# A macaron block in float32 on one core: the attention pass in another order, with other PSUM banks and other places for its transfers

## The reference

```
x = x + 0.5 * ffn(layernorm(x))
x = x + attention(layernorm(x))
x = x + 0.5 * ffn(layernorm(x))

attention, 16 heads of 32:
  q, k = l2_normalize(x Wq), l2_normalize(x Wk);  v = x Wv
  alpha = sigmoid(x Wa + ba);  beta = sigmoid(x Wb + bb)
  for each token:  pred  = state^T k
                   state = alpha * state + k (beta * (v - pred))^T
                   out   = state^T q
  y = rmsnorm(out) * g_norm * silu(x Wg);  return y Wo

ffn, 64 slots:
  h = gelu([x, mean of slots] w1 + b1);  logits = (h w2 + b2) / (|tau| + 0.1)
  weights = softmax over the 8 largest logits, 0 elsewhere
  slots' = GRU(slots, weighted means of x);  out = weights (slots' wv + bv) wo + bo
```

## Time and profile before

| | |
|---|---|
| time, median of 3 runs | 3005.53 us (2997.7 to 3006.02) |
| the profiled execution itself | 2985.76 us |
| its span in the trace | 2983.5 us |
| PE / PEld / DVE / ACT / POOL busy | 91% / 65% / 63% / 35% / 44% |
| mean granted TensorE clock, 1 being 2.4 GHz | 0.961 |
| DMA traffic | 224.78 MB, 75 GB/s on average; 277585 of 365966 packets under 512 bytes |
| largest lines of the chain that ended last | L849 22%, L1052 8%, L906 7%, L1011 5%, L1033 5% |

### The profile page before, as it was taken

How to read it: one execution, slowest core, us unless ns; L and a number is a source line. 1 busy time by engine, 2 the same in 40 slices (tenths; PEclk the granted TensorE clock), 3 DMA queues, 4 the chain that set the end, 5 groups by cost and what they waited for, 6 DMA issues and landing times.

```text
span 2983.5 us, 117215 instructions
## 1 busy us (share of the span) xinstructions
PE 2726.1 (91%) x51052; PEld 1952.7 (65%) x51052; DVE 1869.4 (63%) x5306; ACT 1041.1 (35%) x1962; POOL 1326.6 (44%) x1767
## 2 busy tenths in 40 slices
PE   7999789999999999999999999999999999999877
PEld 6887466666666666666666666666666666666653
DVE  7777456665666666666656666656666666665536
ACT  5776223333333333333233333333333333333320
POOL 2221344554444545444454555544544444455410
PEclk9999899999999999999999999999999999999978
DMA  7342122222112222221222222221212222122168
GB/s 232 94 160 64 37 53 60 61 61 61 40 55 56 61 61 61 61 61 50 52 61 57 57 61 61 61 61 43 55 52 61 61 61 57 52 54 61 49 240 310
DMA packets 365966, 224.78 MB, mean 75 GB/s; under 512 B 277585, under 2 KB 294033, under 8 KB 365457
## 3 DMA queue, kind: packets, MB, share of 16 engines
q1 hardware_dynamic: 356240, 200.51, 23.9%
q10 hardware_dynamic: 9216, 16.78, 1.5%
HBM read 125.49 MB, written 74.97 MB: 67 GB/s over the span
## 4 chain that ended last, share of the span: by engine, by line
PE 81%; DVE 10%; issue 5%; ACT 2%; DMA 1%; SPq 1%; POOL 1%; DVEq 0%; ACTq 0%; POOLq 0%
PE psum L849 22%; PE psum L1052 8%; PE psum L906 7%; PE psum L1011 5%; PE psum L1033 5%; PE psum L970 4%; PE psum L946 4%; PE psum L1020 4%; PE psum L1073 4%; PE psum L690 3%; DVE blk L2627 2%; PE psum L989 2%; PE psum L753 2%; DVE blk L2629 2%; PE psum L927 2%
## 5 line engine op out<-in xcount | busy, mean ns | idle before, releaser
L849 PE MATMUL psum<-w_all,xnT 128*128 128x512 f32 (+2 forms) x2048 | 774.8, 509 | 3.0 <-ACT xnT L1715 2.4
L2064 POOL TENSOR_TENSOR sm<-sm,half 128x1 f32<-128x1 f32 (+1 forms) x384 | 535.4, 1394 | 72.9 <-ACT sm L1759 56.9
L849 PEld LDWEIGHTS psum<-w_all,xnT 128*128 128x128 f32 x2048 | 364.8, 195 | 147.2 <-issue 97.4
L2627 DVE TENSOR_TENSOR blk<-blk 128x30 f32<-128x30 f32 (+14 forms) x960 | 375.4, 391 | 49.5 <-issue 23.9
L2629 DVE TENSOR_TENSOR blk<-blk 128x30 f32<-128x30 f32 (+14 forms) x960 | 351.6, 366 | 33.0
L906 PEld LDWEIGHTS psum<-xnT,w_all 128*128 128x128 f32 x2048 | 262.4, 206 | 49.2 <-issue 47.5
L906 PE MATMUL psum<-xnT,w_all 128*128 128x128 f32 x2048 | 280.2, 294 | 3.2 <-issue 3.2
L1033 PE MATMUL psum<-qg,st 32*32 32x64 f32 x8192 | 186.8, 232 | 98.6 <-DVE st L2646 95.2
L1020 PE MATMUL psum<-pk,uw 32*32 32x64 f32 x8192 | 226.0, 217 | 34.2 <-issue 33.1
L1052 PE MATMUL psum<-w_out,gate 128*128 128x512 f32 x512 | 250.7, 612 | 0.4 <-DVE gate L2651 0.4
L2163 POOL TENSOR_TENSOR sq<-sq 128x256 f32<-128x256 f32 x64 | 47.4, 741 | 453.8 <-ACT sq L1795 453.8
(11 more groups left out here) (278 smaller groups left out, 4738.1 us busy)
## 6 DMA issues: line engine op xcount, KB each, us to landing
blk<-n_scratch SPq DMA_DIRECT2D x64, 512.0 KB, 4.7
xin<-in_L_attn_x_dram SPq DMA_DIRECT2D x96, 256.0 KB, 3.1
n_scratch<-nn SPq DMA_DIRECT2D x64, 256.0 KB, 3.8
xh<-xc SPq DMA_DIRECT2D x64, 256.0 KB, 2.7
e_scratch<-blk SPq DMA_DIRECT2D x32, 512.0 KB, 2.7
E<-e_scratch SPq DMA_DIRECT2D x64, 256.0 KB, 3.9
x_scratch<-xh SPq DMA_DIRECT2D x62, 256.0 KB, 2.1
rxn<-in_L_attn_x_dram SPq DMA_DIRECT2D x32, 256.0 KB, 3.0
```

Source lines behind the costliest of these rows:

```text
L849: last = mm(dst, xnT[b][:, k * P:(k + 1) * P], w_all[:, k * WK + at:k * WK + at + n], start=(k == 0), stop=(k == KC - 1))
L2064: return g.tensor_tensor(dst, a, half[:, 0:n], ALU.pow)
L2627: own(tt(o, Y[:, 0:rows, s_:s_ + 1].to_broadcast([P, rows, cols]), N[:, s_:s_ + 1, s_ + 1:CH].to_broadcast([P, rows, cols]), ALU.mult))
```

## The change

The functions compute the same as before, with the same instructions. Three things are replaced.

- **The table of PSUM banks**, and with it the condition in every `free(...)` of TensorE's functions.
- **The order of the calls** in `step_pe`, `step_act`, `step_dve`, `step_pool` and in the `first_...` and `last_...` lists. The small products of a tile are spread differently among the large ones, and `apply_uw` of the second batch begins in the step before, beside that of the first.
- **The order of the transfers** in `step_sp`.

```diff
-        ffn_at = [banks(0, 1), banks(7, 1)]
-        xT_at = [banks(6, 1), banks(3, 1)]
-        k_at = [banks(4, 1), banks(2, 1)]
...
+        ffn_at = [banks(1, 1), banks(0, 1)]
+        xT_at = [banks(7, 1), banks(7, 1)]
+        k_at = [banks(4, 1), banks(0, 1)]
...
             def out_proj(n, b, part):
                 if part == 0:
                     pe.wait_ge(S["y3"], both(n, b))
                     if b == 0:
-                        free((n + 1, (S["e4"], n + 1)), (n - 1, (S["top"], both(n - 1 + NT, 0))), (n, (S["gate"], both(n, 1))))
+                        free((n + 1, (S["draw"], both(n + 1, 0))), (n, (T["qg"][0], nth(n, 1))))
...
             def logits(n, b):
                 pe.wait_ge(S["hT"], both(n + NT, b))
...
-                    free((n + 2, (S["xnT"], both(n + 2, 0))), (n + 1, (S["vb"], both(n + 1, 1))), (n, (T["qg"][1], nth(n, 1))))
+                    free((n + 2, (S["qn"], both(n + 2, 1))), (n, (S["ysq"], both(n, 1))))
...
             def step_sp(o, p, q, r, s):
-                load_first(p, 0)
-                inverse_in(r, 0)
-                inverse_in(r, 1)
-                coupling_out(q, 0)
+                store_second(r, 0)
+                hold(q, 0)
+                store_alpha(s)
                 load_first(p, 1)
-                coupling_out(q, 1)
-                store_second(r, 0)
-                coupling_in(q)
-                hold(q, 0)
                 store_second(r, 1)
+                load_alpha(o)
                 hold(q, 1)
                 inverse_out(q)
-                store_alpha(s)
-                load_alpha(o)
+                inverse_in(q, 0)
+                inverse_in(q, 1)
+                coupling_out(p, 0)
+                coupling_out(p, 1)
+                load_first(o, 0)
+                coupling_in(p)
```

More of the change, by code:

```diff
@@ L1133, in last_pe @@
                 apply_uw(NT - 2, 1, 3)
+                out_proj(NT - 2, 0, 3)
+                slots(NT - 3)
                 apply_gy(NT - 2, 1, 3)
-                slots(NT - 3)
-                qe_T(NT - 2, 1, 1)
                 apply_gy(NT - 2, 1, 4)
@@ L1235, in last_pe @@
                 apply_uw(NT - 1, 1, 3)
+                out_proj(NT - 1, 0, 3)
+                slots(NT - 2)
                 apply_gy(NT - 1, 1, 3)
-                slots(NT - 2)
-                qe_T(NT - 1, 1, 1)
                 apply_gy(NT - 1, 1, 4)
@@ L1269, in last_pe @@
                 hidden(NT - 1, 1, 1)
-                logits(NT - 1, 1)
+                proj_g(NT, 1, 3)
                 qe_T(NT, 0, 0)
@@ L1301, in last_pe @@
                 apply_uw(NT, 1, 3)
+                out_proj(NT, 0, 3)
+                slots(NT - 1)
                 apply_gy(NT, 1, 3)
-                slots(NT - 1)
-                qe_T(NT, 1, 1)
                 apply_gy(NT, 1, 4)
@@ L1308, in last_pe @@
                 apply_gy(NT, 1, 7)
+                alpha_T(NT - 1)
                 chain(NT, 1, 0)
@@ L1519, in step_pe @@
                 gram(q, 0, 1)
+                dec(q, 0)
                 chain(r, 0, 0)
[L1521 to L1530 removed]
+                gram(q, 0, 2)
+                gram(q, 0, 3)
+                chain(r, 0, 1)
+                dec(q, 1)
+                chain(r, 0, 2)
+                logits(s, 1)
+                cum(q)
+                gram(q, 1, 0)
+                chain(r, 0, 3)
+                qe_T(r, 1, 0)
                 gram(q, 1, 1)
[L1532 to L1533 removed]
                 out_proj(r, 0, 0)
[L1535 removed]
                 gram(q, 1, 2)
@@ L1545, in step_pe @@
                 apply_uw(r, 1, 3)
+                out_proj(r, 0, 3)
+                slots(s)
                 apply_gy(r, 1, 3)
-                slots(s)
-                qe_T(r, 1, 1)
                 apply_gy(r, 1, 4)
@@ L2329, in _ @@
+                key_written(p, 0)
+                slot_add(s)
+                y_power(q, 0)
             first_pool()
@@ new lines, in first_dve @@
+                query_scale(3, 0)
+                key_sums(3, 1)
+                key_turn(3, 0)
+                query_turn(3, 0)
+                chunk_kept(2, 0, 1)
+                query_sums(3, 1)
+                key_scale(3, 1)
+                state(2, 0, 0)
+                key_turn(3, 1)
+                state(2, 0, 1)
+                query_scale(3, 1)
+                query_turn(3, 1)
+                coupling(3, 0, 0)
+                reading(3, 0, 0)
+            def step_dve(o, p, q, r, s):
@@ L2964, in step_dve @@
                 last_top(r, 0)
-                last_top(r, 1)
                 query_sums(p, 0)
                 gates_in(p)
+                key_scale(p, 0)
                 gates_beta(p)
-                key_scale(p, 0)
                 gates_decay(p)
-                last_weights(r, 0)
+                chunk_kept(q, 0, 0)
+                query_scale(p, 0)
+                key_sums(p, 1)
+                key_turn(p, 0)
+                query_turn(p, 0)
+                chunk_kept(q, 0, 1)
+                query_sums(p, 1)
+                key_scale(p, 1)
+                state(q, 0, 0)
+                key_turn(p, 1)
+                state(q, 0, 1)
+                query_scale(p, 1)
+                query_turn(p, 1)
+                coupling(p, 0, 0)
+                reading(p, 0, 0)
             ve.wait_ge(wih_st, RELOAD)
```

1092 lines of the change are left out of this document (526 added, 566 removed).

## The result

The changed kernel takes 2837.95 us (median of 4, 2831.22 to 2844.90), the kernel before on the same chip 3005.78 us (2997.7 to 3019.69): ratio 0.9437, interval 0.9395 to 0.948. The profiled execution took 2835.61 us.

A forecast was written before the change was run, and what follows sets the result against it. TensorE bounds it; only 7.6 of 79.3 us a step (clock 2.2, idle 5.4) can be won. 71.7 + 0.4 + 1.8 + 1.5 + 0.8 = 76.2, so 2912 us; range 2880 to 2945, 8 in 10: 2852 to 3008.

The forecast's parts named there:

- What bounds it: TensorE in the attention pass: of 79.3 us a step, only 7.6 of slow clock and idle time can be won.
- Waits on data: TensorE's waits for other engines' results: 1.8 us a step in sum, for 3.0 now.
- The large item: Wait of chunk 1 of batch 1 for `state` behind the inversion: 0.5 us a step for 3.0 now.
- new short covers: New waits where the order gives up cover: `out_proj` batch 0 +0.4, batch 1 +0.4, chunk 3 +0.3, `logits(s, 1)` +0.1.
- Clock: TensorE's time lost at 1.2 GHz behind gaps: 0.8 us a step for 2.2, bounds 0 and 2.2.
- Runs of small products: TensorE going in and out of two more runs of small products, 0.21 us each: +0.4 us a step.
- the two switches: Two more runs of small products on TensorE, each costing 0.21 us for going in and out.
- Issue: TensorE idle with no visible wait, its instruction supply competing with transfers: 1.5 us a step for 2.4, bounds 0.8 and 2.4.
- Rival A: Instruction supply stays: issue 2.4, clock 1.8, 78.1 us a step, 2970 us; chance 0.20.
- Sum: All terms of a step: 76.2 us for 79.3, over 30 steps -93 us, so 2912 us.
- Rival D: More goes: transfers take 9.6 us, stalls over 1 us disappear; 73.7 us a step, 2838 us; chance 0.12.
- Rival C: Slower: GpSimd's roots pace a loop through all engines; at 5 us too many 3062 us; chance 0.13.

The follow-up runs named there:

- gap_back: Changed kernel with rows 1 to 9 of VectorE's inversion ahead of `state` of chunks 0 to 2 of batch 1: 2969.2 us, ratio 0.9953.
- before_both: Kernel before with `state` of batch 1 moved ahead on VectorE and TensorE's waits thinned to 3073 instructions a step: 2870.5 us, ratio 0.9588.
- lock_p45: Changed kernel with 28 redundant TensorE waits fewer a step (3072 instructions) and 170 satisfied waits once ahead of the pass: 2851.7 us, ratio 0.9528.
- lock_bad: Changed kernel with 28 redundant TensorE waits fewer a step (3072 instructions) and 200 satisfied waits once ahead of the pass: 2761.7 us, ratio 0.9266.
- pool_quiet: Kernel before with GpSimd's `key_decayed` of batch 0 and `slot_add` moved ahead of `chunk_decay(q, 1)`: 2925.5 us, ratio 0.9777.

## Why the prediction was wrong in size

*What bounds it* was right: the step lost 4.7 of the 7.6 us named as clock and idle time, and gap_back gives 4.1 of them back. The split was not quite: the waits over 0.15 us called issue are 2.2 us a step and not 2.4, and they are not always amid 32x64 products (8.6 of their 64.0 us stand before others, lines 836, 906 and 849).

*Waits on data, forecast 1.8, measured under 0.1.* The step that failed. The large item was right in mechanism and too careful: the read lands 8.0 to 9.8 us after `nn`, where I had 9.6 to 11.1; the inversion begins 9.4 us after it in the good steps; its three rows take the 1.5 us that I had put, instead of 3.3; and the cover was enough. The four "new short covers" (0.4 + 0.4 + 0.3 + 0.1) do not exist: no wait of `out_proj` for `gated` and none of chunk 3 shows among TensorE's waits over 0.15 us. VectorE's timeline at the end of `chain` of batch 1 shows why:

```profile
1631.28 0.65 DVE L2529 TENSOR_TENSOR xc<-xin,psum 128x512 f32<-128x512 f32 x1
...
1632.99 0.28 DVE L2647 STREAM_TRANSPOSE st<-psum 128x128 f32<-128x128 f32 x1
1633.20 0.65 DVE L2652 TENSOR_TENSOR gate<-psum,gate 128x512 f32<-128x512 f32 x1
```

I had counted `first_sum`, `reading` and the moments as behind the last `chain`, 2.2 us in all; they ran from 1631.28, while TensorE was still ahead of and in it (it ends at 1632.4), and `gated` was done at 1633.9, before TensorE's two parts of `proj_g` were (1634.4).

*Clock, forecast 0.8, measured 0.2.* The three steps with a fall are busy 73.4 to 73.7 us, the other 26 on average 71.8: 5 us in 29 steps. The cause that I named, the wait for `state`, was right for 18 of the 28 falls before; the other 10 followed stalls that I had counted as idle time alone. With no gap over 2.1 us the clock falls in 3 steps of 29. It stayed up behind all 21 stalls of 1.0 to 1.5 us, and in the step with 6.4 us of stalls in all.

*Runs of small products, forecast +0.4.* Not seen: the shortest step is busy 71.2 us where the full-clock step before had 71.7. Over all steps at full clock it is 71.8 us (26 steps) against 72.1 (3 steps), and 72.3 in before_both (26 steps), which has the old order. Something else in the order must give more than the two switches cost; no run isolates it. The Trainium skill's rule of the drain (TensorEngine Tiling, "Key Properties") would have made the change lose here; the whole step does not show that.

*Issue, forecast 1.5, measured 2.5.* The other step that failed, in the other direction. I had put it down to competing transfers, and moved it with them. It hangs on where borders of 256 instructions fall, which the change left drifting: the same 3100 a step. Rival A had the right value and the wrong reason, and the clock that it expected to fall behind these stalls in many steps fell in three.

*Sum.* 71.7 + 0.4 + 1.8 + 1.5 + 0.8 = 76.2 was forecast. In those terms 71.8 + 0.2 + 2.5 + 0.1 = 74.6 came: work with the switches in it, clock, issue, and other idle time. The 1.6 us too many are some 50 of the 74 us by which 2912 missed. Another 6 are the start and the end of the pass, put at 0. The last 18 are the step from the profiled execution to the median: of the 167.8 us between the medians only 150 lie between the profiled executions, for that of before was 20 us under its median, that of the changed kernel 2 us. Rival D's 73.7 had the clock right, put 0.8 us of waits where there were none, and had issue, at 0.8, wrong; that its 2838 is the measured median is luck, made of this step.

*Rival C* did not occur: no wait of TensorE for a root or `query_scale` shows.

## What to carry to other kernels

A wait of a few us costs more than its length when the clock falls behind it; look at which engine's instruction stands in the way, and test by moving that one. When two kinds of gap bring the clock down, mending one alone gains less than its share. A list of transfers on one queue belongs to one order of the data: swap one without the other and a late store blocks an early read. When an engine idles for nothing that the profile shows, count its instructions modulo 256 at the stalls; if all have the same number, thin redundant waits until a step is a multiple of 256, and try places for the border with a few instructions ahead of the loop: here the bad place cost 3.0 us a step against the best.

## What the runs showed of the hardware

- TensorE's instructions come 256 at a time (405 packets for 103752 rows). In the stalls TensorE resumes about 2.6 us after the start of a packet, and no sooner where no other transfer is in flight (changed kernel); 256 instructions of 32x64 products take 1.99 us (lock_p45).
- 200 instructions of satisfied semaphore waits in a row on TensorE delayed the pass by 23 us, 0.11 us each (lock_bad).
- The granted clock fell in 26 of 29 steps with waits of 3.3 us a step (gap_back), and in 3 of 29 with stalls of up to 2.1 us; behind none of 21 stalls of 1.0 to 1.5 us, behind 3 of 12 longer ones (changed kernel).
- GpSimd's 128x512 instructions of 1.05 and 1.26 us stretch short VectorE instructions beside them: 1.7 us a step of VectorE's busy time went when they were moved (pool_quiet).
